# Two-layer attention and expert kernel: the last four experts taken by token halves, with the next layer's norm and queries of the first half among them

## The reference

```
x = x + cross_attention_0(layernorm(x), context)   # 8 heads of 64
x = x + experts(layernorm(x))                      # 8 experts, top 2 of them per token
x = x + cross_attention_1(layernorm(x), context)   # 16 heads of 8, with biases
x = x + sign_mlp(layernorm(x))                     # 128 -> 512 -> 512 -> 128, weights +1/-1
```

```
combine = top-2 softmax weights of the token, by expert
h = xf @ W1[e];  g = xf @ W2[e]                    # 128 -> 256 each
y = (silu(h) * g) @ W3[e]                          # 256 -> 128
out = sum over e of y * combine[:, e]
```

## Time and profile before

| | |
|---|---|
| median of 3 runs | 241.98 us (241.79 to 243.56) |
| profiled execution | 242.18 us, span 240.4 us |
| busy: PE, DVE, ACT, POOL | 223.1, 169.7, 123.0, 59.9 us |
| granted TensorE clock, mean | 0.998 |

### The profile page before, as it was taken

One profiled execution on the slowest core, in us unless ns is written; L12 is line 12 of the kernel. 1 busy time (PEld: TensorE's weight loads), 2 busy tenths in 40 slices (PEclk: granted clock), 3 DMA queues, 4 the chain that ended last, 5 costly groups with the idle time before them and its releaser, 6 DMA issues.

```text
span 240.4 us, 4941 instructions
## 1 busy us (share of the span) xinstructions
PE 223.1 (93%) x1785; PEld 180.7 (75%) x1785; DVE 169.7 (71%) x438; ACT 123.0 (51%) x292; POOL 59.9 (25%) x87
## 2 busy tenths in 40 slices
PE   8988888989799999999999999999799999699993
PEld 8346677888787888898898899777578887477782
DVE  1699985768747796556555558988778887398752
ACT  2644669697864462212312324255356557547651
POOL 3272195006220124433033900260000000220200
PEclk9999999999999999999999999999999999999999
DMA  6940010000000002202102162000000000000002
GB/s 190 246 110 30 3 44 4 0 3 0 0 3 0 3 1 65 55 12 65 52 16 65 43 175 68 1 0 3 0 4 3 0 3 3 0 3 1 0 0 87
DMA packets 11820, 8.18 MB, mean 34 GB/s; under 512 B 2964, under 2 KB 11096, under 8 KB 11800
## 3 DMA queue, kind: packets, MB, share of 16 engines
q1 hardware_dynamic: 11800, 7.91, 12.6%
HBM read 5.81 MB, written 0.52 MB: 26 GB/s over the span
## 4 chain that ended last, share of the span: by engine, by line
PE 71%; DVE 13%; ACT 9%; issue 3%; DMA 2%; SPq 0%; DVEq 0%
PE ps L626 10%; PE ps L798 9%; PE ps L449 8%; PE ps L451 8%; PE ps L450 8%; ACT probs L907 6%; PE ps L540 3%; PE ps L717 3%; PE ps L745 3%; PE ps L445 3%; PE ps L704 3%; PE ps L520 3%; DMA x_sb<-in_x 2%; PE ps L730 2%; PE ps L758 2%
## 5 line engine op out<-in xcount | busy, mean ns | idle before, releaser
L956 ACT ACTIVATE kT<-ps 128x512 f32<-128x512 f32 x32 | 19.1, 598 | 47.4 <-PE ps L451 47.4
L626 PEld LDWEIGHTS ps<-w,kT 128*128 128x128 f32 x256 | 30.9, 192 | 1.2
L626 PE MATMUL ps<-w,kT 128*128 128x128 f32 x256 | 31.0, 275 | 0.0
L1273 DVE TENSOR_TENSOR kT<-ps,kT 128x512 f32<-128x512 f32 x32 | 21.8, 689 | 11.1 <-PE ps L451 8.8
L1280 DVE SCALAR_TENSOR_TENSOR x_sb<-ps,comb,x_sb 128x128 f32<-128x128 f32 x64 | 18.0, 343 | 13.5 <-PE ps L626 13.5
L449 PE MATMUL ps<-xT_hi,w_hi 128*128 128x512 f32 x64 | 26.7, 417 | 0.8 <-issue 0.6
L451 PE MATMUL ps<-xT_hi,w_lo 128*128 128x512 f32 x64 | 25.2, 393 | 0.0
L450 PE MATMUL ps<-xT_lo,w_hi 128*128 128x512 f32 x64 | 25.0, 390 | 0.0
L907 ACT ACTIVATE probs<-ps,negmax 128x128 f32<-128x128 f32 x64 | 22.7, 420 | 1.8 <-DVE negmax L1198 1.8
L1367 DVE TENSOR_REDUCE probs<-ps 128x8 f32<-128x1024 f32 x16 | 19.4, 1224 | 4.4 <-PE ps L704 4.3
L1002 ACT ACTIVATE probsT<-ps 128x1024 f32<-128x1024 f32 x16 | 16.5, 1029 | 9.7 <-PE ps L717 9.7
(11 more groups left out here) (190 smaller groups left out, 491.6 us busy)
## 6 DMA issues: line engine op xcount, KB each, us to landing
w_raw<-in_L_ffn_W SPq DMA_DIRECT2D x16, 128.0 KB, 2.2
k_st<-h_a SPq DMA_DIRECT2D x12, 128.0 KB, 2.7
w<-in_L_ffn_W SPq DMA_DIRECT2D x8, 128.0 KB, 2.1
x_sb<-in_x SPq DMA_DIRECT2D x1, 512.0 KB, 5.6
out<-qo SPq DMA_DIRECT2D x2, 256.0 KB, 2.4
ctx_sb<-in_ctx SPq DMA_DIRECT2D x1, 384.0 KB, 3.8
w_raw<-in_L_xattn_Wq SPq DMA_DIRECT2D x1, 256.0 KB, 5.8
wo<-in_L_xattn_Wo SPq DMA_DIRECT2D x1, 256.0 KB, 5.7
```

Of the source, the lines that this page charges most:

```text
L626: ins = pe.matmul(ps[:, 4 + slot, k * C:(k + 1) * C], uT[:, slot, c, k * P:(k + 1) * P], w3[:, buf, c, :], start=(c == 0), stop=(c == NH - 1))
L956: act.activation(silu[:, c, :], ps[:, c, :], ACT.Silu).then_inc(b_silu, 1)
L1273: dve.tensor_tensor(uT[:, slot, c, :], ps[:, 2 + c, :], silu[:, c, :], ALU.mult).then_inc(b_u, 1)
```

## The change

The last four experts (4 to 7) are computed first for half 0 of the tokens, all four, and then for half 1 (`LATE`). All four must therefore be in memory at once: experts 6 and 7 get buffers of their own (`W_HI`, `W_LO` in `h_a`, `W_DOWN` in `wo0`), and POOL no longer waits for `b_g` before it splits them. SP's loop ends one turn earlier and the loads of experts 6 and 7 follow it in the order up, down, up, down, without a wait for down products.

Half 0 of the next layer's norm runs inside the second half's experts: root on POOL and scaling on ACT for both halves now, transposes on PE ahead of block 15, the four queries of half 0 in two pairs around down product 14. The last down product writes each batch into a bank of its own and signals it; DVE adds and takes statistics batch by batch. Of the fillers 13 are left in this place out of 25.

```diff
+        W_HI = (w12_hi[:, 0, :], w12_hi[:, 1, :], h_a[:, 1, 0, :], h_a[:, 1, 1, :])
+        W_LO = (w12_lo[:, 0, :], w12_lo[:, 1, :], h_a[:, 1, 2, :], h_a[:, 1, 3, :])
+        W_DOWN = (w3[:, 0], w3[:, 1], wo0[:, 0:NH, :], wo0[:, NH:2 * NH, :])
...
+        LATE = [(e, t) for t in range(NT) for e in range(E - 4, E)]
+        LAST_BANK = (5, 4, 2, 3)
...
-            with sp.Fori(1, E // 2) as i:
+            with sp.Fori(1, E // 2 - 1) as i:
                 for buf in range(2):
                     sp.wait_ge(b_lo, i * 2 + (buf - 1))
                     load_up(i * 2 + buf, buf)
                     sp.wait_ge(b_y, i * 4 + (2 * buf - 2))
                     load_down(i * 2 + buf, buf)
+            sp.wait_ge(a_wo, NB)
+            for buf in range(2):
+                e = E - 2 + buf
+                sp.wait_ge(b_lo, e - 1)
+                load_up(e, buf)
+                load_down(e, 2 + buf)
...
-                if not isinstance(e, int) or e >= 2:
+                if e >= 2 and slot < 2:
                     pool.wait_ge(b_g, e * 4 - 4)
...
-            for b in range(NB):
-                if b == 4:
-                    ln_root(2, 1)
...
+            for t in range(NT):
+                bs = slice(4 * t, 4 * t + 4)
+                ln_root(2, t)
...
+            def b_late_hidden(n):
+                e, t = LATE[n]
+                pe.wait_ge(b_lo, e + 1)
+                b_hidden(E + n, e - (E - 4), t)
...
+            for n in range(5):
+                b_late_down(n)
+                b_late_hidden(n + 2)
+            b_late_down(5)
+            ln_transposes(2, 0)
+            b_late_hidden(7)
             pe.wait_ge(masks, 13)
-            for n in range(NG):
-                c_queries(n)
+            c_queries(0)
+            c_queries(1)
+            b_late_down(6)
+            c_queries(2)
+            c_queries(3)
+            b_late_down(7)
             pe.wait_ge(k1_st, NK1)
-            keep_busy(6, M0)
             c_scores(0, 0)
+            pe.wait_ge(b_acc, 2 * E + 5)
             c_scores(0, 1)
-            keep_busy(5, M0)
+            keep_busy(7, M0)
             c_scores(1, 0)
+            keep_busy(4, M0)
             ln_transposes(2, 1)
-            keep_busy(2, M0)
             c_turn_max(0)
             keep_busy(2, M0)
...
+            b_silu_step(2 * E - 2, (0,))
+            ln_scale(2, 0)
+            b_silu_step(2 * E - 2, (1,))
+            ln_hi_copy(2, 0)
             b_silu_step(2 * E - 1)
-            table(ACT.Exp)
```

More of the change, by code:

```diff
@@ L407, in _ @@
                              is_lo[:, 1:2].to_broadcast([P, NG * NB * P])).then_inc(k1_fill, 1)
-            with pool.Fori(2, E // 2) as i:
-                for buf in range(2):
-                    split_expert(i * 2 + buf, buf)
+            for slot in range(4):
+                split_expert(E - 4 + slot, slot)
             pool.memset(top_w, 0.0).then_inc(zeros_ok, 1)
@@ L416, in _ @@
             pool.tensor_copy(v_a[:, :, :, 0:D1], v1.rearrange("p b (h d) -> p b h d", d=D1)).then_inc(c_v, 1)
-            for b in range(NB):
-                if b == 4:
-                    ln_root(2, 1)
[L421 to L425, removed]
+            for t in range(NT):
+                bs = slice(4 * t, 4 * t + 4)
+                ln_root(2, t)
+                pool.wait_ge(ln_rs, SEEDED[2, t])
+                chain(pool.tensor_tensor(nm[:, bs], meanvar[:, bs, 0], rs[:, bs], ALU.mult))
+                pool.tensor_scalar(nm[:, bs], nm[:, bs], -1.0, None, ALU.mult).then_inc(ln_nm, 1)
+                for b in range(4 * t, 4 * t + 4):
+                    pool.wait_ge(ln_xn, 2 * NB + b + 1)
+                    pool.tensor_tensor(x_sb[:, b, :], x_sb[:, b, :], bo1[:, :], ALU.add).then_inc(xb1, 1)
             for n in D_POOL:
@@ L605, in gate_logits, with b_hidden @@
                        xT_hi[:, t * TG:(t + 1) * TG], xT_lo[:, t * TG:(t + 1) * TG]).then_inc(g_T, 1)
-            def b_hidden(q, buf, t, chunks=range(NH)):
+            def b_hidden(q, slot, t, chunks=range(NH)):
                 for c in chunks:
@@ L948, in _, with b_silu_step @@
             table(ACT.Silu)
-            def b_silu_step(q):
-                for c in range(NH):
+            def b_silu_step(q, chunks=range(NH)):
+                for c in chunks:
                     v = q * NH + c
@@ L977, in _ @@
             table(ACT.Silu)
-            with act.Fori(0, NP - 1) as i:
+            with act.Fori(0, NP - 2) as i:
                 b_silu_step(i * 4 + 2)
@@ L995, in c_query_signed @@
                                scale=sign[:, 0:1]).then_inc(c_part, 1)
-            ln_hi_copy(2, 0)
-            for n in range(NG):
-                c_query_signed(n)
+            c_query_signed(0)
+            c_query_signed(1)
+            table(ACT.Exp)
+            c_query_signed(2)
+            c_query_signed(3)
             def c_exp_half(b, a):
@@ L1046, in d_evacuate @@
                                    scale=scale2[:, layer:layer + 1]).then_inc(d_relu_a, 1)
[L1048 to L1051, removed]
+            ln_scale(2, 1)
             ln_hi_copy(2, 1)
@@ L1326, in _ @@
                 k1_low(t)
-            with dve.Fori(0, NP - 1) as i:
+            with dve.Fori(0, NP - 2) as i:
                 q, e = i * 4, i * 2
@@ L1337, in _, with b_late_add @@
                 b_gate(q + 5, 1)
[L1338 to L1342, removed]
+            def b_late_add(n):
+                e, t = LATE[n]
+                b_add(E + n, n % 2, e, t, E + n + 2 if n % 4 else E + n + 1)
+            b_late_add(0)
+            b_gate(E + 2, 0)
+            b_late_add(1)
+            b_gate(E + 3, 1)
+            b_late_add(2)
+            b_gate(E + 4, 0)
+            b_late_add(3)
+            dve.wait_ge(b_acc, E + 6)
             for b in range(4):
                 ln_stats(b)
[L1345 to L1348, removed]
+            b_gate(E + 5, 1)
+            ln_seed_pool(2, 0)
+            b_late_add(4)
+            b_gate(E + 6, 0)
+            b_late_add(5)
             ln_low(2, 0)
[L1350 to L1353, removed]
+            b_gate(E + 7, 1)
             def c_query_stack(n):
@@ L1443, in d_low @@
                 dve.tensor_tensor(h[:, 1, m, :], relu[:, n % ND, :], f32(h[:, 0, m, :]), ALU.subtract).then_inc(d_lo, 1)
-            for n in range(NG):
-                c_query_stack(n)
+            c_query_stack(0)
+            c_query_stack(1)
+            b_late_add(6)
+            c_query_stack(2)
+            c_query_stack(3)
+            b_last_add(0)
+            for k in range(1, 4):
+                b_last_add(k)
+                b_last_stats(k - 1)
+            b_last_stats(3)
+            ln_seed_pool(2, 1)
             dve.wait_ge(zeros_ok, 1)
```

73 lines of the change are left out of this document (43 added, 30 removed).

## The result

| | before | changed |
|---|---|---|
| median of 9 executions each, taken together | 242.57 us (241.79 to 244.01) | 246.06 us |
| a repeat of the changed kernel, 6 executions | | 246.25 us |
| executions at a mean clock of 0.996 or more, in all comparisons | 241.62 to 242.23 us | 244.23 to 245.15 us |
| ratio | | 1.0092 [1.0053, 1.0131]; repeat 1.0106 [1.0043, 1.0169] |

The forecast of 244.3 us is where the changed kernel lies at full clock. Its two medians are 1.8 and 2.0 us higher, just over the range, because lower clocks are in them: of its 15 executions five took 250.64 to 253.43 us at a mean clock of 0.946 to 0.964. One more took 363.81 us, with a clock that fell near 12 us and stood at 0.50 to 0.56 from 20 us to the end; it is left aside. The ratios compare only executions within 1.5% of their kernel's fastest, and those near 0.95 are counted apart.

A forecast was written before the change was run, and what follows sets the result against it. PE bounds the expert stage, then the second half's norm ends last. Delays of 1.45, 4.36 and 0.55 us put the last down product at 157.4; behind DVE's queue the turn comes 2.3 us later: 244.3 us, range 242.8 to 246.0.

The forecast's parts named there:

- term A: PE's wait near 122 us for expert 6's split weights, plus restart: 1.45 to 1.7 us, taken as 1.45.
- Weights late: Expert 6 is needed two blocks earlier but its loads are not earlier, so PE waits 1.2 to 1.45 us from 121.96.
- The weights come in time: Rival: SP issues expert 6 some 1.4 us earlier, only +0.9 us remains, 242.9 us; chance 12%.
- term C: Two small PE waits around the last hidden block: 0.3 us for the first half's norm, 0.26 restarting queries; 0.55, bounds 0 to 1.0.
- Order on DVE: After the fourth query, DVE's last additions stand behind its stacking; the second half's guess moves from 156.6 to 160.0 us.
- Splitting the additions by batch gains nothing there: At DVE's last additions: product's first part is done 0.45 us after the query, DVE comes 1.5 us after it.
- The sum: All delays up to the end of the turn of the maxima: from 163.66 to 165.97 us, +2.3 us.
- Fillers bring nothing: Between last expert and turn, the twelve fillers removed from PE (2.8 us) win nothing: the wait they covered is longer now.
- PE alone bounds: Rival: second half's norm does not end last, so the removed fillers come off whole, 2.8 us, 239.2 us; chance 5%.
- this sign: Expected in the changed profile: PE's busy time lower by some 2.8 us, with the span higher.
- The clock: PE from 160 to 166 us: full clock kept; rival that it falls adds 2 to 4 us, 246.3 to 248.3, 8%.
- No cover behind the turn: After the turn of the maxima the order is the same in both kernels and nothing absorbs a shift.

The follow-up runs named there:

- bare kernel: Kernel before, own order, with 13 of its 25 fillers taken out: ratio 1.0035 over two executions; the other four took 247.74 to 248.92 us.
- undivided kernel: Changed kernel with the last down product in one bank, one signal, four additions then four statistics, no extra fillers: ratio 1.0416, 251.79 to 254.28 us.
- early kernel: Changed kernel with expert 6's loads issued ahead of the wait for the eighth down product: ratio 1.0031; nine of thirteen executions took 248.97 to 253.46 us.

## Why the prediction was right, and where it was not

Adjusted times of the repeat against the steps of the prediction:

| step | predicted | shown |
|---|---|---|
| POOL ends the split of expert 6 | 123.15 to 123.41 | 124.66 - 1.36 = 123.30 |
| wait and restart, term A | 1.45 (to 1.7) | 1.40 + (0.50 - 0.24) = 1.66 |
| fourth query ends | 155.6 | 156.96 - 1.36 = 155.60 |
| guess of the second half ends | 160.0 | 161.16 - 1.36 = 159.80 |
| ACT's scaling ends | 165.15 | 166.32 - 1.36 = 164.96 |
| turn ends | 165.97 | 167.13 - 1.36 = 165.77 |
| span | 242.7 | 243.9 - 1.36 = 242.5 |

**Weights late: right.** I took the loop's end at 0.66 us per issue and left the restart beside a wait of 1.2; the wait was 1.40 and the restart came on top, so the term sat at its upper bound. Loading expert 6 early took 1.6 us off the turn. "The weights come in time" (242.9) is what the early load gives at full clock: 243.13 and 243.27.

**A small piece of luck.** The fourth query ended at 155.60 as forecast because two errors cancel. Term A was 0.2 us larger, and of term C only the wait of 0.3 was there (the transposes ahead of block 15 end 7.23 us behind block 13, where PE alone has 6.94 to do); the restart of the queries, 0.26, was not.

**Order on DVE: right for the guess, in part for the time.** The additions stood behind the stacking; taking them ahead moved the guess by 1.75 and 1.55 us. In the time this gave some 0.5 us with early loads and fillers (242.32 and 242.42 against one execution at 242.88, all at full clock) and nothing without them. "Splitting the additions by batch gains nothing there, since DVE is late" was too strong: it gains 0.4 us. The sum's own numbers had it: the whole down product ends 1.79 us behind the query and DVE is free after 1.5, so undivided additions wait 0.3, and 0.31 is what they waited.

**Fillers bring nothing: right on the time, wrong on their use.** The sum at full clock needed no gain from the twelve, and nine more cost at most 0.14 us, which refutes the rival that PE alone bounds. PE's busy time did not drop by 2.8 us in the repeat (223.3 against 223.1); part of that is the early low-clock piece, in which each matmul takes longer, so this sign could not be read.

**The clock: the step that failed.** I put the fall at 8% and its price at two to four us. A mean clock below 0.97 came in a third of the changed kernel's executions, and those were 6 to 9 us longer (250.64 to 253.43 against 244.23 at full clock). I reasoned from one stretch of one execution, 204:208, 2.68 busy of 4 at full clock. Such a row can't decide it. Ahead of the falls stand pieces with 0.33 and 0.84 us busy of 2, and in the bare kernel 0.95, with the clock already falling in it; but the repeat kept its clock behind 0.81, and in the attention steps the kernel before kept it behind 0.70, where with four fillers fewer it fell behind 0.74:

```profile
170.00:172.00 2.00, 0.70 (x22) 0.56 (x16) 1.60 (x2) 1.52 (x2) 0.00 (x0) 1.00 0.00 0
172.00:174.00 2.00, 2.00 (x16) 1.62 (x13) 1.51 (x2) 0.50 (x1) 0.00 (x0) 1.00 0.00 0
```

```profile
170.00:172.00 2.00, 0.74 (x9) 0.67 (x10) 1.90 (x3) 1.10 (x2) 0.00 (x0) 1.00 0.00 0
172.00:174.00 2.00, 2.00 (x6) 1.59 (x7) 1.19 (x1) 0.45 (x1) 0.00 (x0) 0.59 0.00 0
```

In these executions it was a matter of chance, which one trace doesn't show and many mean clocks do. And I priced the fall by a few us behind it, where the half level held from 164 to 186 us in the undivided kernel and from 166 to 174 in the early one. The Trainium skill (TensorE: Matmul & The Clock Gate, section What's actually happening) has the gate follow how busy PE was recently, and says that one kernel begins with a different number of slow matmuls from run to run. This case agrees with the first by the fillers, which held the clock, and it shows chance inside a kernel too: the changed kernel's executions had mean clocks from 0.946 to 0.998. The same page's section HAM oscillation shows the trouble with waits for DMA between matmuls. Here it was waits for VectorE, of 1.72 us in the undivided kernel and of 1.05 us in the bare one, with shorter ones around them.

The link from missing fillers to the fall is shown in both orders: without cover 4 of 6 executions are below 0.97 (kernel before, bare), 5 of 14 (changed, the one at 363.81 us aside), 9 of 13 (early) and 6 of 6 (undivided); with it 0 of 6, 0 of 12, 0 of 12, 0 of 6, and 0 of 57 of the kernel before. For the early, the undivided and the bare kernel this is clear of chance, for the changed one taken alone it is not. The kernel with the last down product first had no such cover and 0 of 6 (lowest 0.972), though its profile shows a short fall, so idle pieces make the fall more likely and not certain. Not shown is a fall in a trace of the changed kernel itself, since its profiled execution kept the clock there.

**No cover behind the turn: half right.** A delay goes through whole (turn +2.25 and +2.11, span +2.1; the fastest times, +2.6, are a little more apart than that, which no row explains). An advance doesn't: of the turn 0.78 earlier 0.38 passed, the rest was taken up by DVE's maxima, which were over only then.

## What to carry to other kernels

When work is moved ahead of a producer, price first what the producer's consumer then waits behind on its own queue, and whether the operands that now come first were loaded in the new order: both were plain in the old trace and held to 0.2 us. A filler that wins no time can still hold TensorE's clock. Before one is taken out, look for the idle pieces that it leaves, but don't trust one trace to say that the clock outlives them: time enough executions to see the mean clock of each. Here four fillers could go, thirteen could not, and a fallen clock made an execution 6 to 9 us longer, where the whole reorder cost 2.6.

## What the hardware showed unexpectedly

With PE busy without a break the clock stayed at the 1.2 GHz level for eight us and more (166:174 in the early kernel, 4.00 of 4 busy in both windows at 0.50; 166:178 in the undivided one, 2.00 of 2 busy in each of six windows at 0.50). Almost every kernel also shows, in some executions, a mean clock of 0.97 to 0.99, also the kernel before (0.971 to 0.992 in 49 of 57). In the profiles these are falls of some four to six us outside the stretch from the last expert to the turn: at 18 to 24 us in the repeat, worth 1.36 us at the stage, and at 172 to 176 in the kernel with four fillers fewer. They spread the times of one kernel by up to 4.6 us (241.62 to 246.19) and are why medians here are compared only with their clocks beside them.
